# Finding each node's first edge in two steps, in one stage with the block tables and the attention weights

## The chip, the core and the metric

The kernel runs on one core of a Trainium2 chip. The core has five engines with queues of their own: TensorE (PE in the profile, its weight loads PEld), VectorE (DVE), ScalarE (ACT), GpSimd (POOL) and SyncE (SP), which here issues transfers only. Sixteen DMA engines move data between DRAM and the on-chip memory. Semaphores order the engines. The metric is the device time of one execution in microseconds (us), taken as the median of several runs.

## The reference

A graph of 6,250 nodes (256 features) and 100,000 edges, sorted by their target node `dst`, goes through four layers, each added to its input: a graph attention network of three passes, a mixture of eight experts, a graph convolution, and a second mixture of four experts.

```python
x = x + _L0_gnn_ref(_layernorm(x), edge_index, W0, as0, ad0, b0, W1, ...)   # three attention passes
x = x + _L0_ffn_ref(_layernorm(x)[None], ...)[0]
x = x + _L1_gnn_ref(_layernorm(x), src, dst, edge_weight, W1, b1, W2, b2)
x = x + _L1_ffn_ref(_layernorm(x)[None], ...)[0]
# one attention pass:
e = leaky_relu(al_s[src] + al_d[dst], 0.2)
emax = segment_max(e, dst); ee = exp(e - emax[dst])
alpha = ee / (segment_sum(ee, dst) + 1e-16)
out = segment_sum(alpha[:, :, None] * h[src], dst) + b
```

The passes need tables that depend on `dst` alone: which edges each of 49 tiles of 128 nodes works through, at what place in the sorted list each node's edges begin (`first_edge`), and where runs of equal `dst` end.

## The kernel before

The work is a row of stages. A stage ends with a barrier of all engines and the clearing of its semaphores by POOL (lines 134 to 147), so stages don't overlap. Four of them stand ahead of the first projection of the node features and are the subject here. The edges lie as 782 blocks of 128 (`EC` = 782, `P` = 128); the nodes as 49 tiles (`NT`).

`step_tables` has two blocks of instructions. In the first, SP loads `dst` three times (shifted by one edge), copies it to a DRAM table `t_dst` of 782 rows of 128, loads the edges' sources and weights, and then clears large DRAM areas from a zeroed tile `zsp` (lines 265 to 277). DVE zeroes `zsp`, compares neighbouring edges, and counts for each of 50 tile bounds how many edges lie below it: 50 passes over the whole edge list (line 311), added over partitions by PE (line 398). From the bounds DVE works out which block of edges each step takes (`te_i`), POOL gathers these blocks (`rows_d`, line 288), and PE turns them. In the second block `first_edge` is found: DVE compares 8 steps at a time (line 450, 128 times), PE adds up (line 489), ACT keeps the sums (line 475), and at the end the result is put together in eight rounds (lines 496 to 502) and seven short operations (lines 459 to 466).

`block_tables` writes penalties of the runs to DRAM and reads them back in another layout (`penT`, line 842), takes minima (line 856), turns them and stores them (line 846). `attention_weights` loads the weights of the three attention layers on SP and ACT, and multiplies them by the attention vectors. `norm_stage` comes next; its first instruction on DVE is line 616.

The helper `Chain.link` makes DVE wait for its own last instruction. Stages, in the order in which they are called:

Of the kernel before, what the change touches and what calls it, by code (L numbers as in the profile page):

```python
# [39 lines left out]
P = 128  # L40
# [151 lines left out]
def step_tables(nc, kit, c, a):  # L192


    with kit.stage() as st:
# [7 lines left out]
        below = sb("below", [P, NT + 1])  # L203
# [25 lines left out]
        pcol = ps("pcol", [P, 512])  # L229
        punit = ps("punit", [1, 3, P])  # L230
# [15 lines left out]
        sel = sb("sel", [P, GC, NT])  # L246
        with nc.Block() as block:
            @block.sync
            def _(sp):
# [5 lines left out]
                sp.dma_start(c.t_dst[0:EC, :], e).then_inc(table, 16)  # L255

# [8 lines left out]
                sp.dma_start(c.t_dst[EC:TROWS, :], c.far_i[0:TROWS - EC, :]).then_inc(table, 16)  # L265
# [13 lines left out]
            @block.gpsimd  # L279
            def _(pool):  # L280
                nc.gpsimd.iota(gnum_i[:, :], pattern=[[P, GC]], base=0, channel_multiplier=1).then_inc(numbered, 1)
                nc.gpsimd.iota(c.far_i[:, :], pattern=[[0, P]], base=FAR, channel_multiplier=0).then_inc(numbered, 1)

                pool.wait_ge(chosen, 1)
                pool.wait_ge(table, 2 * 16)
                for k in range(GC):
                    at = bass.IndirectOffsetOnAxis(ap=te_i[:, k:k + 1], axis=0)
                    pool.indirect_dma_start(rows_d[:, k, :], None, c.t_dst, at).then_inc(fetched, 16)

            @block.vector  # L290
            def _(dve):
# [4 lines left out]
                v.memset(zsp[:, :], 0.0).then_inc(numbered, 1)  # L296
# [17 lines left out]
                dve.wait_ge(numbered, 3)  # L314
                ch.link(v.tensor_copy(gnum[:, :], gnum_i[:, :]))
# [3 lines left out]
                ch.link(v.tensor_copy(bound_i[:, :], pcol[:, 0:NT + 1]))  # L319
# [56 lines left out]
                for k in range(GC):  # L376
                    v.tensor_scalar(sel[:, k, :], c.iota[:, 0:NT], tn[:, k:k + 1], None, ALU.is_equal)
# [16 lines left out]

            @block.tensor
            def _(pe):
                pe.wait_ge(counted, 1)
                nc.tensor.matmul(pcol[:, 0:NT + 1], c.ones[:, :], below[:, :], start=True, stop=True).then_inc(summed, 1)
# [15 lines left out]

        step_cols = st.sb("step_cols", [P, GMAX])
        lt = [st.sb(f"lt{b}", [P, 8, P], BF16) for b in range(2)]
        ones_h = st.sb("ones_h", [P, 1], BF16)  # L420
        iota_h = st.sb("iota_h", [P, 1, P], BF16)
        drel_h = st.sb("drel_h", [P, GMAX, 1], BF16)
        inside = st.sb("inside", [P, GMAX], BF16)
        tcol = st.sb("tcol", [P, P + 1])
        at_f = st.sb("at_f", [P, 2, NT])
        pcnt = [st.ps(f"pcnt{b}", [P, 8]) for b in range(2)]
        pfirst = psum[:, 0:2, 0, 0:NT]
        pt = st.ps("pt", [P, P + 1])
        setup, compared, colsum = st.sem("setup"), st.sem("compared"), st.sem("colsum")
        moved, own2, tposed = st.sem("moved"), st.sem("own2"), st.sem("tposed")  # L430
        tkept, found = st.sem("tkept"), st.sem("found")
        passed = [st.sem(f"passed{j}") for j in range(3)]
        NGB = GMAX // 8
        with nc.Block() as block:
            @block.vector
            def _(dve):
                v = nc.vector
                ch = Chain(dve, own2)
                v.memset(ones_h[:, :], 1.0)

                v.tensor_copy(drel_h[:, :, 0], c.drel[:, :])
                v.tensor_scalar(inside[:, :], c.drel[:, :], float(P), None, ALU.is_lt).then_inc(setup, 1)
                ch.link(v.tensor_copy(iota_h[:, 0, :], c.iota[:, 0:P]))
                dve.wait_ge(setup, 1)
                with dve.Fori(0, NGB // 2) as i:
                    for b in range(2):

                        dve.wait_ge(colsum, i * 2 + (b + 1))
                        dve.sem_inc(passed[0], 1)
                        v.tensor_tensor(lt[b][:, :, :], iota_h[:, :, :].to_broadcast([P, 8, P]),  # L450
                                        drel_h[:, ds(i * 16 + b * 8, 8), :].to_broadcast([P, 8, P]), ALU.is_gt
                                        ).then_inc(compared, 1)
                for k in range(GC):
                    dve.wait_ge(tposed, k + 1)
                    if k:
                        dve.wait_ge(found, k)
                    v.tensor_copy(tcol[:, :], pt[:, :]).then_inc(tkept, 1)
                dve.wait_ge(found, GC)
                ch.link(v.tensor_copy(at_f[:, :, :], pfirst[:, :, :]))

                ch.link(v.tensor_tensor(at_f[:, 1, :], at_f[:, 1, :], at_f[:, 0, :], ALU.is_equal))
                ch.link(v.tensor_scalar(at_f[:, 1, :], at_f[:, 1, :], float(FAR), None, ALU.mult))
                ch.link(v.tensor_scalar(pair_f[:, 0:NT], pair_f[:, 0:NT], float(W * P), None, ALU.mult))
                ch.link(v.tensor_tensor(at_f[:, 0, :], at_f[:, 0, :], pair_f[:, 0:NT], ALU.add))
                ch.link(v.tensor_tensor(at_f[:, 0, :], at_f[:, 0, :], at_f[:, 1, :], ALU.add))
                ch.link(v.tensor_copy(c.first_edge[:, :], at_f[:, 0, :]))

            @block.scalar
            def _(act):
                act.sem_inc(moved, 2)  # L470
                with act.Fori(0, NGB // 2) as i:
                    for b in range(2):
                        act.wait_ge(colsum, i * 2 + (b + 3))
                        act.sem_inc(passed[1], 1)
                        nc.scalar.activation(step_cols[:, ds(i * 16 + b * 8, 8)], pcnt[b][:, :], ACT.Copy
                                             ).then_inc(moved, 1)

            @block.tensor
            def _(pe):
                pe.wait_ge(setup, 1)  # L480
                pe.sem_inc(colsum, 2)
                with pe.Fori(0, NGB // 2) as i:
                    for b in range(2):
                        pe.wait_ge(compared, i * 2 + (b + 1))

                        pe.wait_ge(moved, i * 2 + (b + 1))
                        pe.sem_inc(passed[2], 1)
                        for k in range(8):
                            ins = nc.tensor.matmul(pcnt[b][:, k:k + 1], lt[b][:, k, :], ones_h[:, :],
                                                   start=True, stop=True)  # L490
# [1896 lines left out]
```

## Time and profile before

| what | us |
|---|---|
| median of 3 runs (lowest, highest) | 7157.64 (7145.47, 7168.07) |
| profiled execution, its own time | 7147.34 |
| its span in the profile | 7145.7 |
| busy in it: PE, DVE, POOL, ACT | 4557.0, 3504.5, 3477.7, 939.0 |

Times in the profile count from the span's start. A row of a timeline gives start, duration, engine, line, operation, output and input, and in brackets how long the engine stood idle before it and what ended that. Rows of several instructions have a count at their end (x8). A row of stretches gives busy time and count of each engine, the granted clock of TensorE as a share of 2.4 GHz, and how busy the DMA engines were; that share can go a little above 1 since packets overlap.

### The profile page before, as it was taken

How to read it: one execution, taken by the hardware profiler on the slowest of the kernel's cores; microseconds unless marked ns; L12 is line 12 of the kernel's file. 1: busy time of each engine (PE TensorE's matmuls, PEld its weight loads, DVE VectorE, ACT ScalarE, POOL GpSimd, SP SyncE). 2: the span in 40 equal slices, each digit the busy share in tenths (PEclk: the TensorE clock that was granted, in tenths of full speed). 3: DMA queues.
4: the chain of work that ended last, by engine and by line, in shares of the span. 5: the costliest groups of instructions: out<-in, count | busy, mean ns of one | idle time of the engine just before them, and what ended most of it. 6: DMA issues, size and time to landing. Idle time of an engine off the chain costs nothing. (4 is left out here: it accounts for less than half of the span.)

```text
span 7145.7 us, 93760 instructions
## 1 busy us (share of the span) xinstructions
PE 4557.0 (64%) x18341; PEld 3261.5 (46%) x18342; DVE 3504.5 (49%) x8023; ACT 939.0 (13%) x2234; POOL 3477.7 (49%) x3549
## 2 busy tenths in 40 slices
PE   1345566763566664556663499999933556667799
PEld 1223344442344443334442288888822344445344
DVE  9535666665566665556667411111154444446344
ACT  2310000020000002000000233222210000003121
POOL 0067777747777757777771130000046777760000
PEclk9977778886777887777886699999966777888777
DMA  3243333334333324333332321111143333330000
GB/s 125 52 123 104 104 104 104 104 90 123 104 104 104 105 79 134 104 104 104 104 104 72 106 89 48 60 48 60 48 135 108 103 104 103 103 93 26 17 15 15
DMA packets 319720, 632.64 MB, mean 89 GB/s; under 512 B 70272, under 2 KB 200760, under 8 KB 317848
## 3 DMA queue, kind: packets, MB, share of 16 engines
q0 software_dynamic: 173872, 475.54, 23.9%
q1 hardware_dynamic: 138344, 149.65, 6.7%
q10 hardware_dynamic: 7440, 6.82, 0.3%
q14 instruction: 50, 0.41, 0.0%
q8 instruction: 14, 0.23, 0.0%
HBM read 534.38 MB, written 97.76 MB: 88 GB/s over the span
## 5 line engine op out<-in xcount | busy, mean ns | idle before, releaser
L951 POOL DMA_INDIRECT rows<-table,ix x2352 | 2301.5, 979 | 741.6 <-issue 687.5
L1211 PE MATMUL acc<-rows,hot 128*128 x5856 | 1624.1, 435 | 229.6 <-DVE hot L1058 176.7
L1211 PEld LDWEIGHTS acc<-rows,hot 128*128 128x128 f32 x5856 | 1163.9, 211 | 646.1 <-issue 439.0
L1058 DVE TENSOR_TENSOR hot<-iota,drel 128x256 f32<-128x256 f32 x1464 | 618.9, 429 | 567.5 <-PE acc L1211 562.8
L1256 POOL DMA_INDIRECT rows<-emb,ix x784 | 758.6, 968 | 261.2 <-issue 230.3
L1377 PE MATMUL acc<-rows,hot 128*128 x1952 | 574.2, 456 | 345.9 <-DVE hot L1298 328.7
L1052 DVE TENSOR_TENSOR rows<-rows,pw 128x1024 f32<-128x1024 f32 x588 | 712.6, 1212 | 0.0
L1377 PEld LDWEIGHTS acc<-rows,hot 128*128 128x128 f32 x1952 | 423.4, 229 | 480.2 <-issue 408.3
L1949 PE MATMUL p<-w,xT 128*128 128x256 f32 x2496 | 557.2, 382 | 23.3 <-ACT xT L1969 23.3
L1940 PE MATMUL p<-xt,w 128*128 128x256 f32 x2496 | 553.5, 380 | 8.0 <-DMA b<-in_b2all 8.0
L1949 PEld LDWEIGHTS p<-w,xT 128*128 128x128 f32 x2496 | 468.3, 190 | 99.1 <-issue 39.1
L1940 PEld LDWEIGHTS p<-xt,w 128*128 128x128 f32 x2496 | 476.2, 191 | 72.8 <-issue 8.3
L1863 POOL DMA_DIRECT2D w<-in_W1all x9 | 6.5, 718 | 855.0 <-DVEq L1999 843.5
L1969 ACT ACTIVATE xT<-p,b 128x256 f32<-128x256 f32 x624 | 290.1, 473 | 628.4 <-PE p L1940 625.6
L1152 ACT ACTIVATE accs<-acc x228 | 88.9, 390 | 2069.0 <-PE acc L1214 2069.0
L1984 DVE COPY xt<-pT 128x512 f32<-128x512 f32 x79 | 54.6, 691 | 558.1 <-PE pT L1926 558.1
L1995 DVE TENSOR_TENSOR ys<-p,b 128x256 f32<-128x256 f32 x156 | 66.2, 425 | 493.3 <-PE p L1949 493.3
L1298 DVE TENSOR_TENSOR hot<-iota,drel 128x256 f32<-128x256 f32 x488 | 201.7, 425 | 211.5 <-PE acc L1377 210.3
L1176 PE MATMUL pS<-ident,terms 128*112 128x128 f32 x84 | 31.5, 375 | 417.3 <-DVE terms L1079 403.0
L511 POOL DMA_INDIRECT spread<-logit,first_edge x147 | 175.9, 1197 | 218.6 <-ACT logit L1528 148.1
L1079 DVE COPY terms<-rows 128x112 f32<-128x112 f32 x84 | 21.9, 261 | 485.0 <-DMA rows<-table,ix 404.6
L1292 DVE TENSOR_TENSOR rows<-rows,wps 128x1024 f32<-128x1024 f32 x196 | 238.0, 1214 | 9.3 <-DMA rows<-emb,ix 9.2
(381 smaller groups left out, 4813.9 us busy)
## 6 DMA issues: line engine op xcount, KB each, us to landing
rows<-table,ix POOLq DMA_INDIRECT x2352, 2.8
xg<-slots_in SPq DMA_DIRECT2D x79, 256.0 KB, 2.7
slots_out<-ys SPq DMA_DIRECT2D x78, 256.0 KB
table<-hs SPq DMA_DIRECT2D x147, 130.0 KB, 2.0
own_row<-table SPq DMA_DIRECT2D x21, 896.0 KB, 10.1
slots_in<-zsp SPq DMA_DIRECT2D x9, 1664.0 KB, 22.1
xin<-in_x POOLq DMA_DIRECT2D x14, 896.0 KB, 6.3
rows<-emb,ix POOLq DMA_INDIRECT x784
```

The lines of the kernel that those rows point to most:

```text
L511: return pool.indirect_dma_start(c.spread, bass.IndirectOffsetOnAxis(ap=c.first_edge[:, t:t + 1], axis=0), c.logit[:, t, H:2 * H], None, b ...
L951: pool.indirect_dma_start(rows[:, h * GB + k, 0:RW], None, table, bass.IndirectOffsetOnAxis(ap=ix[:, h, k:k + 1], axis=0)).then_inc(landed ...
L1052: v.tensor_tensor(r, r, w.to_broadcast([P, W, H, HD]), ALU.mult).then_inc(weighed, 1)
L1058: v.tensor_tensor(hot[j][:, :, :], c.iota[:, 0:P].rearrange("p (o n) -> p o n", o=1).to_broadcast([P, 2, P]), c.drel[:, ds(q * W + j * 2, ...
L1211: ins = nc.tensor.matmul(A, hot[j][:, k, :], four[:, j * 2 + k, :], start=False, stop=False, skip_group_check=True)
L1256: pool.indirect_dma_start(rows[:, h * GB + k, 0:D], None, table, bass.IndirectOffsetOnAxis(ap=ix[:, h, k:k + 1], axis=0)).then_inc(landed[ ...
L1292: v.tensor_tensor(r, r, w.to_broadcast([P, W, D]), ALU.mult).then_inc(weighed, 1)
L1298: v.tensor_tensor(hot[j][:, :, :], c.iota[:, 0:P].rearrange("p (o n) -> p o n", o=1).to_broadcast([P, 2, P]), c.drel[:, ds(q * W + j * 2, ...
L1377: ins = nc.tensor.matmul(A, hot[j][:, k, :], four[:, j * 2 + k, :], start=False, stop=False, skip_group_check=True)
L1940: ins = nc.tensor.matmul(p1[f % 4][:, :], w1[b][:, k, f * P:(f + 1) * P], xt[:, k, :], start=(k == 0), stop=(k == 1))
L1949: ins = nc.tensor.matmul(p2[t][:, :], hT[:, f, t * P:(t + 1) * P], w2[b][:, f, :], start=(f == 0), stop=(f == FT0 - 1))
L1969: nc.scalar.activation(hT[:, f, :], p1[f % 4][:, :], ACT.Gelu, bias=b1[b][:, f:f + 1]).then_inc(bent, 1)
```

## The change

The two blocks that found `first_edge` and the two stages after them become one stage. `c.last` holds, on every partition, the last `dst` of each of the 782 blocks. A node's first edge is then looked up in two steps: count the blocks whose last `dst` is below the node (that names the block), gather that block from `t_dst`, and count in it the edges below the node.

In `step_tables` the 50 counts over the whole list go too: one two-step lookup, for 128 values at once, takes their place. `c.last` comes from a new transfer `last_i` (782 single words, 512 bytes apart) that PE multiplies onto all partitions and ACT keeps. The zeroing of `zsp` moves from DVE to POOL, and the transfer of the two end rows of `t_dst` moves ahead of the loads of sources and weights. In the joint stage the weights are loaded by ACT alone.

```diff
 step_tables, SP:
                 sp.dma_start(c.t_dst[0:EC, :], e).then_inc(table, 16)
+                sp.dma_start(last_i[:, :], e[:, P - 1:P].rearrange("t o -> o t"), allow_slow_non_contiguous=True
+                             ).then_inc(ends_in, 16)
+                sp.wait_ge(numbered, 2)
+                sp.dma_start(c.t_dst[EC:TROWS, :], c.far_i[0:TROWS - EC, :]).then_inc(table, 16)
...
 POOL:
+                nc.gpsimd.memset(zsp[:, :], 0.0).then_inc(numbered, 1)
+
+                pool.wait_ge(asked, 1)
+                pool.wait_ge(table, 2 * 16)
+                pool.indirect_dma_start(found_i[:, :], None, c.t_dst,
+                                        bass.IndirectOffsetOnAxis(ap=sought_i[:, 0:1], axis=0)).then_inc(answered, 16)
...
 DVE:
-                v.memset(zsp[:, :], 0.0).then_inc(numbered, 1)
+                dve.wait_ge(ends_in, 16)
+                v.tensor_copy(last_f[:, :], last_i[:, :]).then_inc(ends_f, 1)
...
+                dve.wait_ge(ends_kept, 2)
+                ch.link(v.tensor_scalar(junk[:, :], c.last[:, :], edge_at[:, :], None, ALU.is_lt, ALU.add,
+                                        accum_out=sought[:, 0:1]))
+                v.tensor_copy(sought_i[:, :], sought[:, 0:1]).then_inc(asked, 1)
                 dve.wait_ge(loaded, 48)
...
-                for n in range(NT + 1):
-                    ch.link(v.tensor_scalar(junk[:, :], dst_f[:, :], float(P * n), None, ALU.is_lt, ALU.add,
-                                            accum_out=below[:, n:n + 1]))
+                dve.wait_ge(answered, 16)
+                ch.link(v.tensor_copy(found_f[:, :], found_i[:, :]))
+                ch.link(v.tensor_scalar(found_f[:, :], found_f[:, :], edge_at[:, :], None, ALU.is_lt, ALU.add,
+                                        accum_out=sought[:, 1:2]))
+                for k in range(2):
+                    ch.link(v.tensor_scalar(parts[:, k, :], c.ident[:, 0:NT + 1], sought[:, k:k + 1], None, ALU.mult))
                 v.nop().then_inc(counted, 1)
...
 ACT and PE:
+                act.wait_ge(ends_put, 1)
+                for j in range(2):
+                    nc.scalar.activation(c.last[:, j * (EC // 2):(j + 1) * (EC // 2)], plast[:, j, 0:EC // 2], ACT.Copy
+                                         ).then_inc(ends_kept, 1)
...
+                pe.wait_ge(ends_f, 1)
+                for j in range(2):
+                    ins = nc.tensor.matmul(plast[:, j, 0:EC // 2], c.ones[0:1, :],
+                                           last_f[:, j * (EC // 2):(j + 1) * (EC // 2)], start=True, stop=True)
+                ins.then_inc(ends_put, 1)
...
 the second block of step_tables (lines 434 to 503 of before) and attention_weights: removed
...
 block_tables, ACT: the loads of attention_weights, for all three layers; POOL and DVE:
+                for i in range(NB):
+                    pool.wait_ge(asked, i + 1)
+                    for t in range(i * UT, (i + 1) * UT):
+                        pool.indirect_dma_start(found_i[:, t, :], None, c.t_dst,
+                                                bass.IndirectOffsetOnAxis(ap=block_i[:, t:t + 1], axis=0)
+                                                ).then_inc(answered[i], 16)
...
+                def search(i):
+
+                    tiles = slice(i * UT, (i + 1) * UT)
+                    for t in range(i * UT, (i + 1) * UT):
+                        ch.link(v.tensor_scalar(lower[:, :], c.last[:, :], c.node[:, t:t + 1], None, ALU.is_lt, ALU.add,
+                                                accum_out=place[:, 0, t:t + 1]))
+                    v.tensor_copy(block_i[:, tiles], place[:, 0, tiles]).then_inc(asked, 1)
+
+                def count(i):
+
+                    dve.wait_ge(answered[i], UT * 16)
+                    ch.link(v.tensor_copy(found_f[:, :, :], found_i[:, i * UT:(i + 1) * UT, :]))
+                    for k in range(UT):
+                        t = i * UT + k
+                        ch.link(v.tensor_scalar(smaller[:, :], found_f[:, k, :], c.node[:, t:t + 1], None, ALU.is_lt,
+                                                ALU.add, accum_out=place[:, 1, t:t + 1]))
+
+                for i in range(NB):
+                    search(i)
...
+                    if i:
+                        count(i - 1)
                 dve.wait_ge(loaded, 16 * (2 * H + 1))
                 v.tensor_reduce(least[:, :, :], c.penT[:, :, :, :], AX.X, ALU.min).then_inc(reduced, 1)
+                count(NB - 1)
...
```

Here `NB` and `UT` are both 7. In the order of the built program, DVE's first instructions in `step_tables` were, before (`dst_f` is the edge list, `junk` a scratch tile, `below` the 50 counts):

```order
L294 MEMSET rows_i 128x256
L295 MEMSET rows_w 128x256
L296 MEMSET zsp 128x6256
L298 CAST dst_f<-dst_i 128x782
L300 CAST oth_f<-prev_i 128x782
```

and are now, with the waits named (`last_i` and `last_f` are the 782 last values, `found_i` the gathered blocks):

```order
L313 CAST last_f<-last_i 1x782 [waits ends_in_90]
L315 CAST gnum<-gnum_i 128x8 [waits numbered_76]
L316 TENSOR_SCALAR edge_at<-gnum 128x1 [waits dve_own_75]
L317 TENSOR_SCALAR node<-iota,gnum 128x49 [waits dve_own_75]
L318 TENSOR_SCALAR to_next<-iota,gnum 128x128
L320 TENSOR_SCALAR junk,sought<-last,edge_at 128x782 [waits ends_kept_93]
L322 CAST sought_i<-sought 128x1 [waits dve_own_75]
L324 CAST dst_f<-dst_i 128x782 [waits loaded_74]
```

The work on the edge list, which began with line 298, now stands behind the wait for `last_i`. In the joint stage the counts of one group of seven tiles stand behind the search of the next group:

```order
L787 TENSOR_SCALAR lower,place<-last,node 128x782 x7
L789 CAST block_i<-place 128x7
L787 TENSOR_SCALAR lower,place<-last,node 128x782 x7
L789 CAST block_i<-place 128x7
L794 CAST found_f<-found_i 128x896
L797 TENSOR_SCALAR smaller,place<-found_f,node 128x128 x7
L787 TENSOR_SCALAR lower,place<-last,node 128x782 x7
```

So POOL gathers a group's seven blocks while DVE searches for the next group. On SP the new transfer stands in front of the loads and the clearing:

```order
L263 DMA t_dst<-in_dst 16x6256
L264 DMA last_i<-in_dst 1x782x1
L267 DMA t_dst<-far_i 2x128
L272 DMA rows_i<-in_src 128x6x128
L274 DMA rows_i<-in_src 14x128
```

Everything that SP issues after line 264 is queued behind it.

## Rows read from the trace of the kernel before

**Rows 1.** Four stretches, one for each block or stage (us, busy and count by engine).

```profile
0.00:99.10 99.10, 8.60 (x36) 6.45 (x37) 82.56 (x200) 0.02 (x1) 10.16 (x19) 1.00 0.56 224
99.10:263.70 164.60, 56.09 (x1072) 46.66 (x1072) 150.66 (x147) 97.82 (x192) 0.00 (x0) 1.00 0.00 0
263.70:308.10 44.40, 0.55 (x2) 0.13 (x2) 8.61 (x5) 0.00 (x0) 0.00 (x0) 1.00 0.54 91
308.10:329.50 21.40, 8.00 (x36) 7.49 (x36) 2.72 (x8) 0.00 (x0) 0.00 (x0) 1.00 0.22 56
```

**Rows 2.** Groups by line, first 330 us: count, busy, mean ns, idle before.

```profile
L450 DVE TENSOR_TENSOR lt<-iota_h,drel_h 128x1024 bf16<-128x1024 bf16 x128 | 145.4, 1222 | 0.5 <-DVE iota_h L443 0.5
L475 ACT ACT_TABLE_LOAD x64 | 82.1, 1283 | 149.1 <-PE pcnt L489 149.1
```

**Rows 3.** Timeline of the first block: start, duration, engine, line, operation.

```profile
9.99 0.50 DVE L298 CAST dst_f<-dst_i 128x782 f32<-128x782 int32 x1
...
17.96 0.97 DVE L311 TENSOR_SCALAR_CACHE_REDUCE junk<-dst_f 128x782 f32<-128x782 f32 x1
...
21.09 1.23 SPq L275 DMA_DIRECT2D slots_out<-zsp  x1
...
67.47 0.97 DVE L311 TENSOR_SCALAR_CACHE_REDUCE junk<-dst_f 128x782 f32<-128x782 f32 x1
...
69.33 0.21 DVE L319 CAST bound_i<-pcol 128x50 int32<-128x50 f32 x1 [0.36 <-PE pcol L398]
...
70.50 0.27 DVE L326 TENSOR_SCALAR_CACHE_REDUCE le<-gs,gnum 128x49 f32<-128x49 f32 x1
...
72.65 0.27 DVE L326 TENSOR_SCALAR_CACHE_REDUCE le<-gs,gnum 128x49 f32<-128x49 f32 x1
...
73.57 0.17 DVE L332 CAST te_i<-te 128x8 int32<-128x8 f32 x1
73.65 1.58 DVE L334 TENSOR_TENSOR whole_groups<-pair_f,group_at 128x1372 f32<-128x1372 f32 x1
74.03 2.17 POOL L288 DMA_INDIRECT rows_d<-t_dst,te_i  x1 [70.81 <-DVE te_i L332]
...
76.50 0.96 POOL L288 DMA_INDIRECT rows_d<-t_dst,te_i  x1 [0.30 <-issue]
...
85.28 1.33 DVE L377 TENSOR_SCALAR sel<-iota,tn 128x49 f32<-128x49 f32 x8
...
87.45 0.69 DVE L382 CAST rows_r<-rows_d 128x1024 f32<-128x1024 int32 x1
```

**Rows 4.** Timeline from the end of the second block to the projection.

```profile
263.43 0.19 DVE L466 CAST first_edge<-at_f 128x49 int32<-128x49 f32 x1
...
266.71 0.27 DVE L852 MEMSET far<- 2x256 f32 x1 [3.08 <-PEq L140]
...
296.41 7.62 DVE L856 TENSOR_REDUCE least<-penT 112x56 f32<-112x7168 f32 x1 [29.09 <-DMA penT<-pens]
...
304.68 0.38 DVE L858 COPY turned<-pt 28x224 f32<-28x224 f32 x1 [0.65 <-PE pt L864]
...
329.48 0.06 DVE L616 MEMSET eps<- 128x1 f32 x1 [1.25 <-PEq L140]
```

**Rows 5.** DMA packets of three stretches: 272 to 273.6, 312 to 312.5, 276 to 294 us.

```profile
DMA packets 84, 0.00 MB, mean 0 GB/s; under 512 B 84, under 2 KB 84, under 8 KB 84
...
DMA packets 450, 0.02 MB, mean 30 GB/s; under 512 B 437, under 2 KB 450, under 8 KB 450
...
DMA packets 5522, 2.78 MB, mean 154 GB/s; under 512 B 98, under 2 KB 5522, under 8 KB 5522
```

**Rows 6.** DMA issues (count, KB each, median us to landing): 0 to 100, 470 to 500 us.

```profile
slots_out<-zsp SPq DMA_DIRECT2D x1, 2304.0 KB, 37.0
...
rows<-table,ix POOLq DMA_INDIRECT x24, 6.5
```

**Rows 7.** A gather of a later stage beside a long operation of DVE: timeline, 458.9 us.

```profile
458.91 3.13 POOL L951 DMA_INDIRECT rows<-table,ix  x1 [0.30 <-issue]
```

More of the change, by code:

```diff
@@ L413, in _ @@
                     ins.then_inc(turned, 1)
[L418 to L490, printed above, removed]
-                        ins.then_inc(colsum, 1)
-                pe.wait_ge(moved, NGB + 2)
-                for k in range(GC):
-                    if k:
-                        pe.wait_ge(tkept, k)
-                    nc.tensor.transpose(pt[:, 0:P], step_cols[:, k * P:(k + 1) * P], c.ident[:, :])
-                    nc.tensor.matmul(pt[:, P:P + 1], inside[:, k * P:(k + 1) * P], ones_h[:, :],
-                                     start=True, stop=True).then_inc(tposed, 1)
-                    pe.wait_ge(tkept, k + 1)
-                    for m in range(2):
-                        ins = nc.tensor.matmul(pfirst[:, m, :], tcol[:, m:m + P], sel[:, k, :],
-                                               start=(k == 0), stop=(k == GC - 1), skip_group_check=True)
-                    ins.then_inc(found, 1)
@@ L813, in block_tables @@
-def block_tables(nc, kit, c):
     with kit.stage() as st:
@@ L824, in block_tables @@
         reduced, put, kept, bounced = sem("reduced"), sem("put"), sem("kept"), sem("bounced")
+        avec = sb("avec", [P, L, 2, 2 * H])
+        wt = [sb(f"wt{l}", [P, 2, D]) for l in range(L)]
+        pw = [ps(f"pw{l}", [P, 2, 2, P]) for l in range(L)]
+        pa = ps("pa", [P, L, 2, 2 * H])
+        w_loaded = [sem(f"w_loaded{l}") for l in range(L)]
+        clear, w_turned, w_kept, prod, done = sem("clear"), sem("w_turned"), sem("w_kept"), sem("prod"), sem("done")
+        lower = sb("lower", [P, EC])
+        place = sb("place", [P, 2, NT])
+        block_i = sb("block_i", [P, NT], I32)
+        found_i, found_f = sb("found_i", [P, NT, P], I32), sb("found_f", [P, UT, P])
+        smaller = sb("smaller", [P, P])
+        lastrow = sb("lastrow", [1, P])
+        pnext = ps("pnext", [P, 2, NT])
+        alike = sb("alike", [P, 2, NT])
+        first_f = sb("first_f", [P, NT])
+        own, asked, placed, shifted = sem("own"), sem("asked"), sem("placed"), sem("shifted")
+        answered = [st.pool_sem(f"answered{i}") for i in range(NB)]
         with nc.Block() as block:
@@ L851, in _ @@
                 v = nc.vector
+                ch = Chain(dve, own)
                 v.memset(far[:, :], -BIG).then_inc(filled, 1)
@@ L865, in _ @@
                 ins.then_inc(put, 1)
+                pe.wait_ge(placed, 1)
+                for k in range(2):
+                    nc.tensor.matmul(pnext[:, k, :], c.to_next[:, :], place[:, k, :], start=True, stop=False)
+                    ins = nc.tensor.matmul(pnext[:, k, :], lastrow[:, :], c.bound[0:1, k, 1:NT + 1],
+                                           start=False, stop=True)
+                ins.then_inc(shifted, 1)
 def attention_pass(nc, kit, c, table, accs):
```

144 lines of the change are left out of this document (77 added, 67 removed).

## The prediction, as recorded before the run

> **What bounds the kernel now.** I read the stretches first, since the four pieces of work that the change touches stand at the very front and follow each other through barriers. Until 329.5 us PE is busy for 73 us in all, and each stretch has another limit [rows 1]. From 0 to 99.1 us DVE is the limit, busy 82.6 us. From 99.1 to 263.7 us it is DVE again, 150.7 of 164.6 us, while no transfer runs and POOL is idle; the groups by line say with what: 128 comparisons of 1222 ns, 145 us together [rows 2]. From 263.7 to 308.1 us the engines mostly wait for transfers. From 308.1 to 329.5 us it is loads and a little PE. Nothing of the projection starts before 329.48 us, POOL's loads included, so a microsecond taken from any of these stretches is a microsecond of the kernel, as long as the later stages take what they took. That is the view to hold on to: this is a serial prefix, and shares of busy time over the whole span say nothing about it.
>
> **The part removed.** The second block goes whole. Its first instruction stands behind a barrier at 99.1 us, its last on DVE ends at 263.43 + 0.19 = 263.62 us [rows 4]: 164.5 us go. Behind it 3.1 us of barrier and clearing pass until the next stage's first instruction at 266.71; these stay, now behind the first block.
>
> **The first block.** The 50 counts run from 17.96 us to 67.47 + 1.01 = 68.48 us, 49 periods in 49.51, that is 1.01 us each for 782 elements with an accumulated sum [rows 3]. They go, and so does the zeroing by DVE, which held line 298 back until 9.99. What comes in their place is a chain that begins with `last_i`, and that transfer is the unknown.
>
> The single-word transfer of the trace, two copies of 28 words in 272 to 273.6 us, made 84 packets, 42 each: 28 words and 14 more [rows 5]. I read the 14 as one completion packet for each engine that took part, two words per engine: equal shares, not 16 engines of which some get more. 782 is 2 x 17 x 23, so equal shares over at most 16 engines leave 2 engines with 391 words each. For the pace of one engine, 450 packets, nearly all of one word, passed in 0.5 us over 16 engines, 18 ns each; strided pieces of 512 bytes passed 5522 in 18 us over (again 28 rows) 14 engines, 46 ns each [rows 5]. So 391 words take 7 us at the one, 18 us at the other, and with 16 engines it would be 49 words and 1 us. I take 7, from the row with words of the same size, and keep 1 and 18 as ends.
>
> The Trainium skill speaks to this: "DMA: Bandwidth & Descriptors", section "Why a DMA increments its semaphore by 16 and not by 1", has a transfer use the largest number of engines, at most 16, that divides its slowest dimension, which is 14 for 28, as the row shows, and 2 for 782. By it the sum stands; without it, with 16 engines, the kernel would end some 6 us earlier. No run so far shows a transfer of 782 pieces.
>
> The chain then, in us from the start. The words queue behind the loads of `dst`, whose conversion shows them in place by 9.99 at the latest; they start near 8.7, end at 15.7 and are seen near 17.2. Converting, two products of 391 columns, a table load of 1.28 [rows 2] and two copies by ACT, with the semaphores between, come to an estimated 4.5: 21.7. Count and conversion, 1.2: 22.9. Now the edge work follows, 17.96 - 9.99 = 8.0: 30.9. It covers the first gather, which POOL starts at 23 and which lands late, because the clearing of DRAM keeps all DMA engines busy: a gather beside heavy traffic took 6.5 us to land [rows 6], and one beside a long two-input operation of DVE took 2.17 instead of 0.96 to issue [rows 3]. I put its answer at 33, two us after the edge work. Turning it into bounds, with one product, 2.4: 35.4, the place of line 319, which was at 69.33. From there to 99.1 it is 29.8, less 1.25 for line 377: 28.5. But line 382 needs the eight gathers of line 288. Before, they had landed when it was reached at 87.45. Now `te_i` is ready at 39.8, POOL issues for 2.17 + 0.30 + 7 x 1.26 = 11.3 until 51.3, and they land beside the clearing near 57. DVE reaches line 382 at 52.3 and waits 5. The first block ends at 35.4 + 28.5 + 5 = 69.
>
> The clearing ends the block as well, for SP waits for it. Before, it landed at 21.09 + 37.0 = 58.1 [rows 3, 6], hidden behind DVE. Two of its engines now start 7 later and all carry nine small gathers: about 66. So the block ends at 69, against 99.1: 30 us less. With `last_i` at its ends, 1 and 18 us, both limits move along: 62 to 80. The zeroing on POOL costs nothing, as the clearing waits behind the loads anyway; if POOL took twice DVE's time, the clearing would start 2 or 3 us late, still within 69.
>
> **The joint stage.** Before, it took 329.48 - 266.71 = 62.8 us. Now DVE is its limit. Five small first instructions, 0.95. A search of seven tiles, 7 x 1.01 + 0.2 = 7.3. A count: converting 896 elements 0.6 (1024 took 0.69), and seven sums over 128 elements; 49 elements have a period of (72.65 - 70.50)/7 = 0.31, 782 of 1.01 [rows 3], so 128 take 0.38: 3.3 in all. Seven of each: 74.2. Copies of the weights, 2.6 (DVE's whole work in the last stretch was 2.72 [rows 1]); the minima of line 856, 7.6 [rows 4], which waited 29 us for its transfer and won't now. POOL needs 7 x 1.26 = 8.8 per group and DVE 10.6, so POOL keeps up, except at the first group: asked at 8.3, issued until 17, landed at 23 beside the transfers of `penT`, while DVE has nothing to do from 15.6. That is 7. After the last count: sums, `turned` 0.4 and four short operations, 2.3 more, ending at 94.8; the store of `turned` and the barrier then take 3.1 as before, from 93.1 on: 96.2 us, against 62.8: 33.4 more. The weights' loads, split over two queues, filled a stage of 21.4 us [rows 1]; from one queue they take less than twice that, and their first use stands at 44.
>
> If the reading of the counts held POOL back, the cover would be gone. A single-input sum beside gathers does not do so: line 326's form ran beside them, and so did the reduction after line 334, with the gather at 76.50 at its usual 0.96 [rows 3]. The Trainium skill says the same, in "SBUF — State Buffer", section "Who interferes with whom", and says that conversions within on-chip memory do hold GpSimd's port: by that, seven conversions of 0.6 would cost POOL 4 us in all, within its slack.
>
> **The sum.** -164.5 - 30 + 33.4 = -161. The profiled execution took 7147.3: 6986. It lay 10 us below the median of its runs, near the lowest, and I go about half of that way: 6990. The later stages are left as they are; TensorE's granted clock there moves between its two levels, and three runs of one program spread over 23 us, so some 10 us either way are not the change's.
>
> **The rivals.**
>
> Gathers behind the clearing. If the first lookup gets through only when the clearing is done, its answer comes at 67 and the block ends near 67 + 2.4 + 28.5 = 98: the whole gain of the first block is lost, 7015 to 7020. For it speaks that the DMA engines are full then; against it the 6.5 us of gathers beside other traffic [rows 6]. 9 in 100.
>
> POOL as the joint stage's limit. One gather beside an operation of DVE took 3.13 + 0.30 [rows 7]. If the search does that to all 49, they take 168 us, the stage near 190, and the kernel 7080. Against it: single-input sums did not do so above. 5 in 100.
>
> Slower: the words of `last_i` one at a time. All DVE work of the block waits for them. If each word costs a full trip instead of following the last closely, at 0.5 us they are seen at 205 instead of 17 us, and the kernel comes to 6986 + 188 = 7174. The point from which it decides is 161/391 = 0.41 us a word. Against it stand 18 and 46 ns. 2 in 100.
>
> Given back later. The tables would be ready earlier, but the passes could meet another pattern of the clock: 7010 to 7030, 4 in 100. That the removed block is replaced at equal cost, so that nothing changes, would need 160 us in places where I count 63: 2 in 100.
>
> **How the numbers follow.** The forecast has 78 in 100, with a range of its own from 6965 to 7010. With the first rival and the later loss taken in, 6955 to 7032 leaves out the other cases and little else. A difference of 0.3%, 21 us, is about what can be told from no change. Faster by more than that: forecast, both first rivals and the later loss, 0.96; same 0.02; slower 0.02.
>
> **What would show it.** No line 450 and no table loads between stages. DVE waiting at the first line of the block for `last_i` until about 17 us; the projection's first instruction near 169 us. In the joint stage a busy DVE with one wait of some 7 us, at the first conversion of gathered blocks. In the first block DVE waiting at the conversion of `rows_d`. Wrong would be: `last_i` landing after 28 us; a gap of DVE at each count; the block's end set by the clearing well after 80 us; or a projection that starts near 169 us and a kernel that is not 150 us faster all the same.

## The result, and the profile after

The changed kernel takes 7004.07 us (median of 4 runs, 6996.92 to 7009.14), the kernel before 7158.93 us beside it (4 runs): a ratio of 0.9784, 95% interval 0.9772 to 0.9796, or 155 us less. The forecast was 6990, its range 6955 to 7032. The profiled execution took 6996.92 us, its span 6995.3.

The prefix up to the projection has two stretches now instead of four [rows 1]. Stretches of the changed kernel (us, busy and count of PE, PEld, DVE, ACT, POOL, then granted clock, DMA share, GB/s):

```profile
0.00:62.10 62.10, 10.36 (x40) 6.48 (x41) 31.11 (x105) 2.19 (x4) 16.44 (x21) 1.00 0.88 359
62.10:165.40 103.30, 11.62 (x46) 9.46 (x46) 84.79 (x229) 0.00 (x0) 46.98 (x49) 0.51 0.37 82
```

In the first block DVE is busy half the time, where it was busy 82.56 of 99.10 us; the DMA share of the stretch is 0.88, where it was 0.56. In the joint stage DVE has 84.79 of 103.30 us.

The timeline of the first block after (start, duration, engine, line, operation; in brackets the idle time ahead and what ended it):

```profile
4.92 0.77 SPq L264 DMA_DIRECT2D last_i<-in_dst  x1
5.74 4.94 SPq L267 DMA_DIRECT2D t_dst<-far_i  x1
...
13.00 0.56 DVE L313 CAST last_f<-last_i 1x782 f32<-1x782 int32 x1 [9.46 <-DMA last_i<-in_dst]
...
17.53 1.03 DVE L320 TENSOR_SCALAR_CACHE_REDUCE junk<-last,edge_at 128x782 f32<-128x782 f32 x1 [3.24 <-ACT last L427]
...
19.04 1.16 POOL L298 DMA_INDIRECT found_i<-t_dst,sought_i  x1 [10.59 <-DVE sought_i L322]
...
23.79 1.31 SPq L286 DMA_DIRECT2D slots_out<-zsp  x1
...
26.71 0.23 DVE L337 CAST found_f<-found_i 128x128 f32<-128x128 int32 x1
...
29.40 0.19 DVE L349 CAST bound_i<-pair_f 128x50 int32<-128x50 f32 x1
...
34.06 2.05 POOL L304 DMA_INDIRECT rows_d<-t_dst,te_i  x1 [13.86 <-DVE te_i L362]
...
51.38 0.69 DVE L410 CAST rows_r<-rows_d 128x1024 f32<-128x1024 int32 x1 [5.15 <-DMA rows_d<-t_dst,te_i]
...
61.26 0.43 DVE L419 COPY ew<-psum 128x272 f32<-128x272 f32 x1
64.50 0.33 SPq L730 DMA_DIRECT2D pens<-pen_fwd  x1
64.61 0.27 DVE L777 MEMSET far<- 2x256 f32 x1 [2.92 <-PEq L140]
```

Two of the block's issues (count, KB each, median us to landing):

```profile
slots_out<-zsp SPq DMA_DIRECT2D x1, 2304.0 KB, 38.6
...
rows_d<-t_dst,te_i POOLq DMA_INDIRECT x8, 7.3
```

The bounds that stood at 69.33 [rows 3] stand at 29.40, and the conversion of `rows_d` at 51.38 instead of 87.45, now with a wait in front of it. DVE ends at 61.69. The last clearing transfer, issued at 23.79, lands 38.6 us later at 62.4: the block's end is set by the clearing, with DVE 0.7 us ahead of it. The next stage's first instruction stands at 64.61, not 266.71 [rows 4].

The timeline of the joint stage:

```profile
88.37 0.63 DVE L794 CAST found_f<-found_i 128x896 f32<-128x896 int32 x1 [7.86 <-DMA found_i<-t_dst,block_i]
...
148.58 7.62 DVE L814 TENSOR_REDUCE least<-penT 112x56 f32<-112x7168 f32 x1
...
162.83 0.19 DVE L827 CAST first_edge<-first_f 128x49 int32<-128x49 f32 x1
165.36 0.06 DVE L565 MEMSET eps<- 128x1 f32 x1 [2.34 <-PEq L140]
```

One wait of 7.86 us at the first count, none at the other six, none for `penT`, where line 856 had waited 29.09 us [rows 4]. No run keeps the two old stages apart, so what joining them gives by itself is read from this wait alone. The projection starts at 165.36 instead of 329.48: 164.1 us earlier. The spans differ by only 150.4, the medians by 155. So 14 us of the profiled execution, 9 by the medians, are given back behind the prefix; the experiments below find most of them.

### The profile page after: what moved, and what is told of

It reads as the page before. It is cut to its first block and busy times, and to the rows that moved or that the text cites. A ratio compares the mean times of both kernels' runs of the same rounds, so it can differ in the third digit from the quotient of the medians.

```text
span 6995.3 us, 90025 instructions
## 1 busy us (share of the span) xinstructions
PE 4522.6 (65%) x17281; PEld 3227.7 (46%) x17282; DVE 3378.3 (48%) x7997; ACT 843.2 (12%) x2045; POOL 3535.6 (51%) x3600
```

## Experiments

Each kernel starts from the changed one. Ratios are to runs of the kernel before on the same chip; the changed kernel's is 0.9784, so 0.001 is 7 us.

**The changed kernel again.** No edit.

> The changed kernel once more, unedited. The prefix up to the projection took 165.4 us in its first profile, 164.1 less than before, but the profiled span was only 150.4 us shorter: 14 us were given back between the attention passes and the end, in three places (4.7 us in the stage behind the attention passes, 8.8 in the expert stage, 4.4 near the end). Theory (the loss is scatter of a single execution): the prefix comes out at 165.4 within 1 us, the extra 14 us sit in other places or are gone, and the median stays near 155 us below before. Rival (an earlier start gives a lasting loss of some 10 us): the same three places are again 4 to 9 us longer than in the kernel before.

7006.94 us (5 runs), before 7161.64, ratio 0.9784 (0.9770 to 0.9797), again 155 us less; projection at 165.9. The expert stage was long again, and so was the stretch near the end (894.6 us after 895.7, against 891.2). The first of the three places, behind the attention passes, was 1.7 us longer instead of 4.7. So the loss is not one execution's scatter, though one of its three parts varies.

**The words in 15 shares, and in one.** `last_i` was split into 780 and 2 words, and into 773 and 9:

```diff
-sp.dma_start(last_i[:, :], e[:, P - 1:P]...).then_inc(ends_in, 16)
+sp.dma_start(last_i[:, 0:780], e[0:780, P - 1:P]...).then_inc(ends_in, 16)   # or 773
+sp.dma_start(last_i[:, 780:EC], e[780:EC, P - 1:P]...).then_inc(ends_in, 16)
```

> The 782 words of last_i in two transfers, 780 and 2, so that 15 equal shares are possible instead of 2. Theory A (the words are limited by the two engines that carry them, near 6 ns a word and engine): the words pass in under 1 us, SP is held far less than 4.94 us behind the issue, and DVE's first instruction on last_i stands near 11 instead of 13.0 us. Theory B (the limit is the making of 782 descriptors, whatever engines carry them): SP is held about 4.9 us again and DVE's first instruction stays at 13 us or comes up to 1 us later for the second transfer.

> The 782 words of last_i in two transfers, 773 (a prime, so only one engine can take equal shares) and 9. Theory A (limited by the engines that carry the words): 773 words at 5.8 ns take 4.5 us instead of 2.3, and DVE's first instruction on last_i stands near 15.3 instead of 13.0 us. Theory B (limited by the making of the descriptors): SP is held about 4.9 us as before and DVE starts within 1 us of 13.0.

Packets while nothing but the words passes, 9 to 10.5 us: first the changed kernel, then the kernel with 773 words.

```profile
DMA packets 514, 0.00 MB, mean 1 GB/s; under 512 B 514, under 2 KB 514, under 8 KB 514
```

```profile
DMA packets 258, 0.00 MB, mean 1 GB/s; under 512 B 258, under 2 KB 258, under 8 KB 258
```

514 packets in 1.5 us against 258: exactly half. With two engines and one, that is 5.8 ns a word and engine in both. The Trainium skill's rule in "DMA: Bandwidth & Descriptors", section "Why a DMA increments its semaphore by 16 and not by 1" (the largest number up to 16 that divides the slowest dimension: 2 for 782, 1 for the prime 773), agrees with these two counts. What SP waits behind the transfer goes the same way. Its issues after the words, with 773 and with 780 first:

```profile
5.75 7.01 SPq L266 DMA_DIRECT2D last_i<-in_dst  x1
```

```profile
5.93 0.65 SPq L266 DMA_DIRECT2D last_i<-in_dst  x1
```

The next issue is held 7.01, 4.94 and 0.65 us with 1, 2 and 15 shares: theory A for the pace and the hold. The hold contains a wait: with two shares SP's next issue begins at 5.74, and the words pass only from about 8.6 us on, when the loads of `dst` are through. DVE's start moved less than A said: 13.9 with one share (15.3 expected), 12.55 with 15 (11 expected). It says little, for with two shares it lay anywhere from 11.8 to 13.4 in the ten traces of the changed kernel and its variants, 12.0 in the repeat. With 15 shares SP is free early, and the loads of `rows_i` and `rows_w` pass beside the words; no packet under 512 bytes passes from 10 to 11 us, so the words are through by then, and what DVE waits for until 12.55 is not shown. The last transfer of the clearing lands at 61.8 instead of 62.4, and the projection stands at 164.6, 0.7 us earlier. With one share the words pass by 13.5, but everything behind is late: the clearing's last transfer lands at 65.4 and the projection stands at 169.0, 3.6 us later. Single runs of 6999.80 us (15 shares) and 7004.20 us (one) can't tell these from the changed kernel. So the price of a narrow transfer of words is mostly its hold on the queue, and from two shares to 15 it is under 1 us of the prefix.

**The counts put back.** The 50 counts in place of the lookup, the rest as changed:

```diff
-ch.link(v.tensor_scalar(junk[:, :], c.last[:, :], edge_at[:, :], None, ALU.is_lt, ALU.add, accum_out=sought[:, 0:1]))
-v.tensor_copy(sought_i[:, :], sought[:, 0:1]).then_inc(asked, 1)
+for n in range(NT + 1):
+    ch.link(v.tensor_scalar(junk[:, :], dst_f[:, :], float(P * n), None, ALU.is_lt, ALU.add,
+                            accum_out=below[:, n:n + 1]))
```

> The first block's lookup undone: the 50 counts over 782 elements of the kernel before take its place, with the loads, the copy of the words and the joint stage as changed. It splits the saving of the first block from the rest. Theory (all DVE work of the block is serial, so the counts cost what they take): 50 x 1.01 us come back, less the wait for the words, the lookup's own count and the wait for the gathers, and the first block ends near 106 instead of 62.4 us, the joint stage is unchanged, the kernel is slower than the changed one by some 44 us (near 7049). Rival (the clearing of DRAM would have ended the block anyway, so the lookup saved little): the block ends below 80 us and the kernel loses less than 20 us.

7039.70 us, ratio 0.9845 (0.9830 to 0.9860): 44 us slower than the changed kernel at the same ratio scale. DVE's last instruction of the block ends at 105.56, the next stage starts at 107.56 instead of 64.61, and the joint stage takes 100.5. The clearing hides nothing of the counts; the rival falls. The lookup in place of the counts is thus worth 43 us, with the copy of the words paid in both. The whole block, which now waits for those words, ends 37 us earlier than before (62.1 against 99.1).

**Searches two groups ahead.**

```diff
-for i in range(NB):
+search(0)
+for i in range(1, NB):
     search(i)
     ...
-    if i:
-        count(i - 1)
+    if i > 1:
+        count(i - 2)
+count(NB - 2)
```

> Joint stage alone: the searches run two groups ahead of the counts instead of one, so the gather of a group has two searches (14.6 us) to be issued and to land. Theory (DVE is the limit of the stage and its only wait for data is the 7.86 us at the first count): that wait goes to under 0.5 us, no other appears, the stage takes 93.3 instead of 100.75 us and the kernel is 7 us faster, a difference that the profile shows and the times hardly can. Rival (POOL's gathers or their landing limit the stage): the wait moves to later counts and the stage gains less than 3 us.

6995.10 us, ratio 0.9770 (0.9755 to 0.9785). The trace is plain where the times are not:

```profile
88.61 0.63 DVE L794 CAST found_f<-found_i 128x896 f32<-128x896 int32 x1 [0.16 <-DMA found_i<-t_dst,block_i]
...
158.03 0.06 DVE L565 MEMSET eps<- 128x1 f32 x1 [2.34 <-PEq L140]
```

The wait of 7.86 is 0.16, no other came, and the projection starts 7.3 us earlier. DVE is the limit of the stage. The times have the difference within their scatter, as expected.

**A constant in the search.**

```diff
-ch.link(v.tensor_scalar(lower[:, :], c.last[:, :], c.node[:, t:t + 1], None, ALU.is_lt, ALU.add,
+ch.link(v.tensor_scalar(lower[:, :], c.last[:, :], float(P * t + 64), None, ALU.is_lt, ALU.add,
```

> The changed kernel with a constant of the instruction in place of a value per partition as the compared number of the 49 searches (so the first edges are not those of the reference, and the later passes read other rows). It asks why one sum over 782 elements had a period of 1.07 us in the search, when it was 1.01 in the removed counts. Theory (reading the compared value from memory costs the 0.06): the period falls to 1.01 and the joint stage shrinks by 3 us. Rival (the period comes from where the sums or the row are kept): it stays at 1.07.

The line's instructions in the changed kernel and here (shortest, median, longest ns):

```profile
L787 DVE TENSOR_SCALAR_CACHE_REDUCE lower<-last,node x49: 1007/1027/1029, 65.3 to 144.0; 128x782 f32<-128x782 f32 x49
```

```profile
L787 DVE TENSOR_SCALAR_CACHE_REDUCE lower<-last x49: 949/968/969, 66.0 to 143.2; 128x782 f32<-128x782 f32 x49
```

1027 against 968 ns: comparing with a value per partition cost 0.06 us each, 2.9 us in the stage. But the stage fell by 1.1 us only. The waits for gathers, one of 7.9 us before, are three here, 9.4 us in all:

```profile
DVE found_f L794 <- DMA found_i<-t_dst,block_i: 9.4, 3, 8.3
```

DVE is 0.4 us faster per group, and the gathers are late. But the edit changes the gathers too: with a constant, all 128 partitions of a gather ask for the same block, and a gather lands in 3.5 us here, where it took 2.5 (medians). Which of the two makes them late is not separated. In the changed kernel the slack is small in any case: the last gather of the sixth group is issued at 142.22, lands some 2.6 us later, and its count begins at 145.20. The half of the theory on the period holds, that on the stage falls. The 5% rival of the forecast, in which the search slows the gathers, is not what shows: beside the searches most gathers are issued in 0.94 us (0.96 in [rows 3]). The single run took 6998.16 us.

**The clearing in the joint stage.** The searches ahead, and the clearing moved behind the loads of `penT`:

```diff
 # first block, SP and POOL
-sp.dma_start(c.spread..., zsp...)       # and 8 transfers to slots_in, slots_out
-nc.gpsimd.memset(zsp[:, :], 0.0)
 # joint stage, behind the loads of penT
+nc.gpsimd.memset(zsp[:, :], 0.0).then_inc(zeroed, 1)
+sp.wait_ge(zeroed, 1)
+sp.dma_start(c.spread..., zsp...)       # and the 8 others
```

> The searches two groups ahead, and the clearing of the slots in DRAM moved from the first block into the joint stage, behind the loads of penT. Theory (in the first block the clearing sets the end and makes the gathers of rows_d land late): the wait of 5.15 us at the conversion of rows_d falls under 1.5 us, DVE ends the block near 57.5 instead of 61.7, nobody waits for the clearing, the joint stage starts near 59.7 and keeps the 7 us that the searches ahead gave; the kernel gains 12 us on the changed one (near 6993). Rival (the clearing only takes its cost along): the gathers of the joint stage land late, counts wait for them, and the joint stage grows by 5 us or more.

6990.23 us, ratio 0.9776 (0.9763 to 0.9790), by the ratio some 6 us better than the changed kernel where 12 were expected. The first block went as expected, the joint stage did not:

```profile
45.55 0.69 DVE L394 CAST rows_r<-rows_d 128x1024 f32<-128x1024 int32 x1 [0.48 <-DMA rows_d<-t_dst,te_i]
...
59.04 5.31 POOL L765 MEMSET zsp<- 128x6256 f32 x1 [15.35 <-POOLq L140]
...
59.75 4.67 DVE L781 TENSOR_SCALAR lastrow<-iota 1x128 f32<-1x128 f32 x1
59.84 4.59 DVE L787 TENSOR_SCALAR_CACHE_REDUCE lower<-last,node 128x782 f32<-128x782 f32 x1
60.78 3.64 DVE L787 DVE_READ_ACCUMULATOR lower<-last,node 128x1 f32 x1
...
158.30 0.06 DVE L549 MEMSET eps<- 128x1 f32 x1 [2.48 <-PEq L140]
```

`rows_d` is waited for 0.48 us and the stage starts near 59.1, 5.5 us earlier. It then takes 99 us, where the searches ahead alone left 93. Neither the theory nor the rival had the first reason: a tiny operation, 128 elements on one partition, takes 4.67 us instead of 0.16 while POOL zeroes, and the first sum is stuck behind it until POOL ends at 64.35. "SBUF — State Buffer", section "Who interferes with whom", in the Trainium skill has this: a tensor-scalar without accumulator may take a port pair that it shares with GpSimd, and whoever comes second is blocked for the whole instruction. The rows agree. The gathers were waited for by 2.5 us as well, the rival's part.

**What is lost behind the prefix: the place of SP's loop.** The expert stage, before and in the changed kernel, in the columns of the stretches above:

```profile
4091.20:5236.50 1145.30, 1119.60 (x5254) 972.58 (x5255) 119.13 (x233) 317.17 (x640) 102.03 (x114) 1.00 0.18 59
```

```profile
3929.50:5083.60 1154.10, 1119.26 (x5255) 971.22 (x5256) 119.31 (x233) 317.17 (x640) 101.57 (x113) 1.00 0.18 58
```

It takes 8.8 us more, at the same granted clock and with the same work on PE. In it PE runs 78 groups at 14.8 us each without slack. In the changed kernel it waits for a group's input `xg` where one routed expert follows another. One such change, first in the kernel before:

```profile
4839.92 0.39 SPq L1893 DMA_DIRECT2D slots_out<-ys  x1
4840.56 0.71 POOL L1863 DMA_DIRECT2D w<-in_W1all  x1 [145.28 <-DVEq L1999]
4840.85 0.38 SPq L1888 DMA_DIRECT2D xg<-slots_in  x1
4841.27 0.92 POOL L1863 DMA_DIRECT2D w<-in_W2all  x1
...
4846.00 0.63 PE L1926 MATMUL pT<-ident,xg 128*128 128x128 f32 x4
```

The same change in the changed kernel:

```profile
4683.37 0.39 SPq L1883 DMA_DIRECT2D slots_out<-ys  x1
4684.00 0.71 POOL L1853 DMA_DIRECT2D w<-in_W1all  x1 [146.43 <-DVEq L1989]
4684.50 0.38 SPq L1878 DMA_DIRECT2D xg<-slots_in  x1
4684.71 0.92 POOL L1853 DMA_DIRECT2D w<-in_W2all  x1
...
4691.31 0.63 PE L1916 MATMUL pT<-ident,xg 128*128 128x128 f32 x4 [1.79 <-DMA xg<-slots_in]
```

From SP's store to POOL's first weights it is 0.63 to 0.64 us in both. From the store to the load of `xg` it is 0.93 before and 1.13 after, in the median of all rounds too, though SP's instructions in this loop are the same. By theory the later load has more of the 2 MB of weights ahead of it. At the seven changes of expert in each of three traces (before, changed, and padded as below), a load issued 0.3 us behind the first weights is never waited for, one 0.5 us behind costs 1.1 to 1.8 us, one 0.8 us behind 1.3 to 1.7, and one a whole microsecond behind 2.4 or more. What differs is where the loop stands: SP has 27 instructions fewer ahead of it. So they were put back as waits long satisfied:

```diff
+for k in range(54):          # two waits to an instruction
+    sp.wait_ge(cuts, 32)
```

> The changed kernel with 27 instructions on SP that do nothing (waits long satisfied), in the joint stage, while SP has nothing to do. They put SP's loop of the expert stage at the same place in its program as in the kernel before, where SP had 27 instructions more ahead of it. Theory (the loss behind the prefix comes from where that loop stands: its jump back and first instructions took 0.2 us longer, the load of xg is issued 0.3 us later and falls behind the weights of the next expert): the issue of xg stands 4.9 instead of 4.6 us ahead of its use, PE's waits for xg fall from 13.1 (7 gaps) to near 2.7 us (2 gaps), the kernel gains 8 to 10 us. Rival (the loss has to do with the time at which the stage runs, or with chance): the issue stays at 4.6 and the waits at 11 to 14 us.

PE's waits for `xg` over the routed experts (us in total, times, longest): before, changed, padded.

```profile
PE pT L1926 <- DMA xg<-slots_in: 2.7, 2, 1.4
```

```profile
PE pT L1916 <- DMA xg<-slots_in: 13.1, 7, 3.1
```

```profile
PE pT L1918 <- DMA xg<-slots_in: 3.2, 2, 1.7
```

The load is issued 4.9 us ahead of its use again, and 9.9 of the 10.4 us are back. In the two runs with the words in two transfers SP had one instruction more: 4.7 us ahead, waits of 11.4 and 11.1. In five other traces with the loop at the changed kernel's place (the repeat, the counts put back, the searches ahead, the constant, the late clearing) the waits are 11.4 to 13.7, though the stage begins up to 43 us later or 6 earlier, so the time at which it runs does not decide. That the loop's place in SP's program does is shown. How is not: "Runtime: NRT & Kernel Launch", section "Instruction fetch mechanics", in the Trainium skill has a taken branch wait for a fetch when its target is outside what is loaded, but the trace has no instruction packet at all between 4308 and 5132 us, 53 rounds of the loop. The time, 6994.03 us from 2 runs (ratio 0.9780, 0.9762 to 0.9798), can't tell 10 us from none.

**The load of `xg` ahead of the store.**

```diff
 load(0)
-with sp.Fori(0, SHG - 1) as g:
-    load(g + 1)
+load(1)
+with sp.Fori(0, SHG - 2) as g:
+    load(g + 2)
     store(g)
 ...                          # and the routed loop in the same way
```

> The changed kernel with SP's loop of the expert stage reordered: the load of the group after next is issued ahead of the store of this group instead of behind it, so some 10 us before its use instead of 4.6, and ahead of the weights of the next expert. Theory (the load of xg loses the race with 2 MB of weights at the change of experts): all of PE's waits for xg, 13.1 us, go but for at most one, and the kernel gains 11 to 13 us on the changed one (near 6993). Rival (what PE waits for there are the weights or the DMA engines in any case): the waits move to the first matmul of the next expert and the gain is under 4 us.

6986.45 us, ratio 0.9771 (0.9758 to 0.9785), 9 us better. The load is issued 13.8 us ahead of its use, PE's waits for `xg` over the routed experts are gone from the list (13.1 before), and the first matmuls of an expert wait for no weights.

**Together.** The searches and the load of `xg` ahead; and the same with the late clearing, whose zeros POOL now makes in the first block, while DVE waits for the words:

```diff
+c.zero = accs[:, :, :].rearrange("p a b -> p (a b)")[:, 0:EC * 8]     # held through both stages
+nc.gpsimd.memset(c.zero, 0.0).then_inc(numbered, 1)                   # first block, POOL
```

> Searches two groups ahead and the load of xg ahead of the store, the clearing where it was: the projection starts near 158.2, PE waits for xg less than 1 us in the expert stage, and the kernel is 18 to 20 us faster than the changed one (ratio to before near 0.9757). If the two edits shared a cause, or if one gave back what the other gains, it would be 12 us or less.

> Together: searches two groups ahead, the load of xg ahead of the store, and the clearing of the slots in the joint stage, but with its zeros made by POOL in the first block, while DVE waits for the words (in the run 'late' POOL made them in 5.3 us at the start of the joint stage, and DVE's first sum there took 3.64 us longer to read its accumulator). Theory (POOL's zeroing beside DVE is what the late clearing cost): the joint stage starts near 59.5, its first sums run at 1.07 us, it takes 93 to 95 instead of 99.2 us, the projection starts near 154 instead of 158.4; with the expert stage's 12 us the kernel is 23 us faster than the changed one (ratio to before near 0.975). Rival (the clearing's transfers slow the gathers, whoever makes the zeros): DVE waits 4 us or more for gathers, the projection starts no earlier than 157.

The first: 6977.87 us, ratio 0.9756 (0.9743 to 0.9769), 20 us better than the changed kernel; projection at 158.0, no wait for `xg`. The two edits add up. The second: 6972.91 us, ratio 0.9751 (0.9738 to 0.9765), the fastest of all. In its joint stage the sums run at once, and the projection starts at 154.5:

```profile
59.85 0.16 DVE L779 TENSOR_SCALAR lastrow<-iota 1x128 f32<-1x128 f32 x1
59.94 1.01 DVE L785 TENSOR_SCALAR_CACHE_REDUCE lower<-last,node 128x782 f32<-128x782 f32 x1
60.89 0.07 DVE L785 DVE_READ_ACCUMULATOR lower<-last,node 128x1 f32 x1
...
154.53 0.06 DVE L550 MEMSET eps<- 128x1 f32 x1 [2.41 <-PEq L140]
```

The stage takes 95.3 us: POOL's zeroing was 3.9 of the 6 us, the gathers' 2.1 us of waiting are the rest. The rival, 4 us of such waits or more, falls.

**The kernel before, profiled again.**

> The kernel before, profiled a second time: every statement on what the later stages lost rests so far on a single trace of it. If the loss is of the program and not of one execution, PE's waits for xg in the expert stage are again near 2.7 us in 2 gaps and SP issues the load 4.9 us ahead of its use. For the stretch of 891.0 us near 5488 to 6379 us, where the changed kernel took 895.7 at a granted clock of 0.79 instead of 0.80: again within 1 us of 891 at 0.80 if the program sets it, anything from 890 to 896 if it is scatter.

7142.65 us. Waits for `xg` 2.5 us in 2 gaps, the load 4.9 us ahead: the program's, not one execution's. The stretch near the end, in the two traces of the kernel before and in the changed one:

```profile
5488.10:6379.30 891.20, 547.67 (x1891) 391.81 (x1890) 392.88 (x708) 26.44 (x69) 677.89 (x700) 0.80 0.36 103
```

```profile
5484.40:6374.60 890.20, 547.81 (x1889) 392.62 (x1887) 393.00 (x707) 26.45 (x69) 676.69 (x701) 0.80 0.36 103
```

```profile
5334.60:6230.20 895.60, 559.61 (x1890) 400.61 (x1889) 393.24 (x708) 26.45 (x69) 682.37 (x700) 0.79 0.36 103
```

PE is busy 547.7 and 547.8 us before and 559.6 after (557.7 to 559 in three of the kernels above), at a granted clock of 0.80 and 0.79; the stretch takes up to 6 us more. That too goes with the program: a slightly longer stretch, from the first to the last operation of ACT there, takes 970.7 and 969.8 us at 0.80 in the two traces of the kernel before, and 972.2 to 976.6 at 0.79 in all twelve of the changed kernel and its variants. Why the clock is granted differently there was not settled.

## Why the prediction was right, and where it was off

The time lay in the range, 14 us above the forecast. The prefix gained 3 us more than the sum had (164.1 against 161), the later stages gave back 14 in the profiled execution, and the median lay 7 us above that execution where the forecast had put 4. Step by step:

- The removed block, and DVE as the limit of the joint stage: right. Four stretches became two.
- `last_i` seen at 17.2: it was 13.0. The two shares were right, the pace was mis-sized: 5.8 ns a word, not 18, so 2.3 us and not 7. The row it came from [rows 5] was of words spread over 16 engines, which was no measure of what one engine can do. Not foreseen: SP held for 4.94 us, which put the clearing's last issue at 23.79 instead of 21.09.
- The chain from there to the count, 4.5: it was 4.53, in part by luck. ACT's table load, 1.28 of it in the prediction, ran at 2.86 us while ACT had nothing else to do, outside the chain; PE took 2.97 us for the products. Count and conversion 1.2, edge work 8.0: 1.22 and 8.0.
- The first gather covered but for 2 us: covered entirely (line 337 has no wait), by little: issued at 19.04, it landed 7.4 us later, and its answer was used at 26.71.
- A wait of 5 for `rows_d`: 5.15, and the first gather's issue 2.05 (2.17 taken). Gathers landed in 7.3 us beside the clearing; moved away from it, in 2.5. So the rival of gathers held until the clearing ends was wrong by size, not by kind.
- The block's end at 69, set by DVE with the clearing at 66: it was 62.4, set by the clearing. DVE's end came 7 us early, 4 of them from the words and 2 from the first gather; the clearing's end came 4 us early.
- The joint stage 96.2: 100.75. The wait of 7 was 7.86. 2.9 us come from the compared values (1.07 for the 1.01 taken), some 2 from the end of the stage: behind the last count DVE waits 1.81 us for PE and the stage ends 5.8 us after it, not 3.7. Conversions and copies of the weights were taken some 1 us too long. The seven conversions cost POOL little: a gather issued beside one took 1.07 to 1.32 us instead of 0.94, under 1 us in all where the prediction had 4.
- Projection near 169: 165.4. The start of the stage was 7.5 early and the stage 4.5 long, so the sum hid 4.5 us of each; that it came so near was luck.
- The step that failed is "The later stages are left as they are". Their source is, their time was not: 9 us by the medians (155 of 164). Most of it, 8.8 us in the expert stage, is the load of `xg` behind the weights, which hangs on 0.2 us of SP's loop; putting the loop back to its place took the waits from 13.1 to 3.2 us. The rival "given back later" had the right effect, 7010 to 7030 was too much, and its reason, another pattern of the clock, holds at most for the smaller part.

## What to carry to other kernels

A transfer of single words costs by the words per engine and can hold the issues behind it on its queue, so look at how many shares its length gives and put what must go out early ahead of it. Here one share instead of two cost the prefix 3.6 us, and 15 instead of two would save 0.7. When a large change lands a few microseconds short, compare the later stages group by group in two traces of each kernel: a loop that runs without slack beside a queue race can shift by its place in the program alone, and issuing the small load earlier removes the race. Move a cost only together with a look at whom its engine disturbs in the new place.

## What the runs showed of the hardware that was not expected

- 782 single words on two engines: 5.8 ns a word and engine; the next issue on SP held 4.94 us (7.01 with 773 words on one, 0.65 with 780 on 15).
- A sum over 782 elements that compares with a value per partition: 1027 ns, with a constant 968.
- POOL zeroing 128x6256 held a DVE operation on 128 elements for 4.67 us instead of 0.16.
- SP's four-step loop: 0.93 or 1.13 us from the store's issue to the next load's, by its place in the program.
